# First products of the experts as fp32r products of a rounded half and a remainder, in a deformable convolution with eight experts

## What is computed

```python
# B, C, H, W = 4, 64, 16, 16
def block(x):
    x = x + conv(_ln_c(x))           # deformable 3x3 convolution, 9 taps, bilinear sampling
    t = x.reshape(B, C, H*W).transpose(0, 2, 1)
    t = t + ffn(_ln_t(t))            # per token, over its 64 channels
    return t back in (B, C, H, W)

def ffn(x):                          # 1024 tokens, 8 experts, hidden 256
    top_w, top_i = top_k(x @ Wg + bg, 2)
    w_dense = sum(one_hot(top_i, 8) * softmax(top_w)[..., None], axis=1)
    out = 0
    for e in range(8):
        h = gelu(x @ W1[e] + b1[e])                  # first product: 64 -> 256
        out = out + w_dense[:, e:e+1] * (h @ W2[e] + b2[e])
    return out
```

## Time and profile before

| | us |
|---|---|
| median of 3 runs (108.62 to 109.21) | 108.91 |
| the profiled execution | 108.63 |
| its span | 106.8 |
| TensorE busy in it | 97.6 |
| VectorE busy in it | 69.3 |
| ScalarE busy in it | 50.7 |

### The profile page before, as it was taken

The page is one execution under the profiler, slowest core; times in us unless marked ns, Lnnn a source line. Parts: engine busy times, 40 slices in busy tenths (PEclk is TensorE's granted clock), DMA queues, the critical chain, the costliest instruction groups (busy, mean ns, idle before and its releaser), DMA issues.

```text
span 106.8 us, 1840 instructions
## 1 busy us (share of the span) xinstructions
PE 97.6 (91%) x624; PEld 53.4 (50%) x624; DVE 69.3 (65%) x196; ACT 50.7 (47%) x99; POOL 13.9 (13%) x25
## 2 busy tenths in 40 slices
...
PEclk9999999999999999999999999999999999999999
...
GB/s 73 179 125 367 5 3 0 6 0 0 0 0 6 0 0 0 0 3 6 0 0 0 0 3 0 6 0 0 0 0 0 0 0 6 0 0 0 0 0 98
DMA packets 1976, 2.37 MB, mean 22 GB/s; under 512 B 816, under 2 KB 1456, under 8 KB 1968
## 3 DMA queue, kind: packets, MB, share of 16 engines
...
...
HBM read 2.00 MB, written 0.26 MB: 21 GB/s over the span
## 4 chain that ended last, share of the span: by engine, by line
PE 73%; DVE 13%; issue 6%; ACT 3%; DMA 2%; POOL 1%; DVEq 0%; POOLq 0%
PE taps_ps L674 16%; PE bank_y L746 14%; PE bank_o L688 14%; PE hid_ps L734 9%; PE taps_ps L734 6%; ACT a_sb L350 2%; DMA xt<-in_x_tok 2%; PE hid_ps L661 2%; DVE a_sb L568 2%; PE bank_p L711 2%; DVE xn L529 2%; PE bank_c L724 2%; DVE at L460 2%; PE bank_p L696 1%; PE bank_p L724 1%
## 5 line engine op out<-in xcount | busy, mean ns | idle before, releaser
L674 PE MATMUL taps_ps<-ident,at 128*128 128x128 f32 x144 | 22.5, 283 | 1.6 <-ACT a_sb L350 1.0
L674 PEld LDWEIGHTS taps_ps<-ident,at 128*128 128x128 f32 x144 | 15.5, 142 | 11.0 <-issue 5.0
L460 DVE TENSOR_TENSOR at<-haty,hats 128x768 f32<-128x768 f32 x22 | 20.6, 951 | 0.1
L688 PE MATMUL bank_o<-a_sb,v_sb 128*64 128x256 f32 x144 | 18.1, 386 | 0.6 <-DVE a_sb L568 0.4
L350 ACT ACTIVATE a_sb<-taps_ps 128x512 f32<-128x512 f32 x22 | 12.9, 592 | 7.8 <-PE taps_ps L674 7.8
L382 ACT ACTIVATE hid<-hid_ps,b_col 128x512 f32<-128x512 f32 x20 | 13.1, 682 | 7.3 <-PE hid_ps L734 7.3
L746 PE MATMUL bank_y<-hid,w_sb 128*64 128x512 f32 x64 | 15.4, 604 | 0.0
L594 DVE SCALAR_TENSOR_TENSOR tmp<-bank_y,b_col,spread 128x512 f32<-128x512 f32 x8 | 6.0, 750 | 13.4 <-PE bank_y L746 13.4
L266 POOL TENSOR_TENSOR rs<-ve,power 128x2 f32<-128x2 f32 (+1 forms) x6 | 5.5, 916 | 65.6 <-DVE ve L475 61.4
L688 PEld LDWEIGHTS bank_o<-a_sb,v_sb 128*64 128x64 f32 x144 | 9.8, 136 | 7.1 <-issue 3.2
L568 DVE COPY a_sb<-taps_ps 128x512 f32<-128x512 f32 x14 | 9.5, 686 | 3.0 <-PE taps_ps L674 2.9
...
## 6 DMA issues: line engine op xcount, KB each, us to landing
w_sb<-in_w SPq DMA_DIRECT2D x2, 512.0 KB, 4.1
...
```

The source lines that it names most:

```text
L460: dve.tensor_tensor(at[:, u % AT_RING, j, :, :].rearrange("p k (y x) -> p k y x", x=W), haty[:, b % 2, j, k0:k0 + GROUP, :].unsqueeze(3).b ...
L674: last = pe.transpose(t_bank(step)[:, st * HW + j * P:st * HW + (j + 1) * P], at[:, u % AT_RING, j, k, st * P:(st + 1) * P], ident[:, :])
L688: last = pe.matmul(bank_o[st * O:(st + 1) * O, 0:HW], v_sb[:, img, st, k, :], a_sb[:, slot % A_RING, st, :], start=(k == 0), stop=(k == TA ...
```

## The change

W1 is loaded twice, onto both halves of the partitions, all eight experts side by side. ScalarE rounds it to fp32r (`w1_hi`, four steps whi), and VectorE subtracts to get what is left (`w1_lo`, four steps wlo). Of the tokens, xs now writes x2s as fp32r, rounded, on all partitions, and a new VectorE step xlo overwrites partitions 64 to 127 with the remainder. An H is then, for each of the two experts, two products with all 128 rows accumulated in one bank: `w1_hi` and `w1_lo`, each with the rounded tokens in the upper rows and their remainder in the lower. H waits for wlo and xlo in place of the load and xs. gate reads the same x2s as fp32 over 128 rows, with its weights doubled. xn1 and xn2 become one buffer, ya loses a dimension. The orders of all four engines and the banks are laid anew; which engine makes a copy changes too: osv1 and one more vs are on VectorE, which has 16 of the E copies where it had 14, and xfl1 in place of xfl3. ACT_ORDER has the steps whi2 (behind tanhm1 and ahead of om2), whi1 (behind E2, ahead of abs1), whi0 and whi3 (behind E10 and tanhm2); its beginning is now "xpl0 xfl0 om0 vs0.0 xpl1 vs0.1 abs0 tanhm0 om1 vs1.0 xpl2 vs1.1 xfl2 tanhm1 whi2 om2 E2 whi1 abs1 xpl3". T19 and T20 are both in bank 0 in the new HOMES.

```diff
 PE_ORDER = (
-    "xnT0 conv0 V0.1 omT0 xnT1 V0.0 conv1 V1.1 omT1 T0 xnT2 T1 xnT3 T2 V1.0 M0 T3 T4 conv2 conv3 T5 omT2 T6 T7 V3.0 T8 omT3 T9 M1 "
-    "T10 V2.1 T11 M2 T12 T13 oT0 T14 M3 T15 T16 M4 T17 V2.0 T18 M5 T19 oT1 T20 xT0 T21 M6 T22 xT1 T23 V3.1 T24 gate0 T25 H0.0.0 "
-    "M7 T26 H0.0.1 T27 M8 H0.1.0 T28 wdT0 T29 oT2 T30 sp0.1 T31 M9 H0.1.1 T32 sp0.0 T33 sp0.2 T34 xT2 T35 M10 O0.0 M11 H0.2.0 oT3 "
-    "H0.2.1 O0.1 H0.3.0 xT3 sp0.3 H0.3.1 gate1 O0.2 H1.0.0 H1.0.1 O0.3 H1.1.0 wdT1 H1.1.1 sp1.0 sp1.1 H1.2.0 O1.0 H1.2.1 sp1.2 "
-    "sp1.3 H1.3.0 O1.1 H1.3.1 O1.2 Fa0 O1.3 Fa1 F0 F1 "
+    "xnT0 conv0 V0.0 omT0 xnT1 V0.1 conv1 V1.0 xnT2 omT1 V1.1 T0 conv2 T1 V2.1 T2 omT2 T3 xnT3 T4 M0 T5 T6 M1 T7 T8 conv3 T9 T10 "
+    "V2.0 T11 M2 T12 omT3 T13 V3.1 T14 T15 oT0 T16 M3 T17 M4 T18 M5 T19 V3.0 T20 oT1 T21 M6 T22 xT0 T23 xT1 T24 M7 T25 H0.0.0 T26 "
+    "gate0 T27 M8 T28 H0.0.1 T29 oT2 T30 wdT0 T31 H0.1.0 T32 M9 O0.0 M10 T33 sp0.2 sp0.0 T34 H0.1.1 T35 sp0.1 xT2 M11 H0.2.0 oT3 "
+    "H0.2.1 O0.1 H0.3.0 xT3 H0.3.1 O0.2 H1.0.0 gate1 H1.0.1 sp0.3 H1.1.0 O0.3 H1.1.1 wdT1 H1.2.0 sp1.0 O1.0 sp1.1 H1.2.1 sp1.2 "
+    "O1.1 H1.3.0 sp1.3 H1.3.1 O1.2 Fa0 O1.3 Fa1 F0 F1 "
 ).split()
...
 DVE_ORDER = (
-    "stats0 xn0 stats1 xpu0 sums0 base0 xn1 pos0 dist0 xpu1 xn2 relu0 haty0 first0 xn3 first1 pos1 first2 xpu2 pr1.0 pr1.1 dist1 "
-    "pr2.0 xpu3 xfl3 E4 pr2.1 relu1 haty1 pr3.0 E6 pr3.1 pos2 dist2 E9 pr4.0 pos3 relu2 pr4.1 pr5.0 dist3 E11 pr5.1 E12 st0 haty2 "
-    "vs2.1 pr6.0 E16 E15 pr6.1 pr7.0 E17 pr7.1 lna0 relu3 pr8.0 st1 pr8.1 E21 lna1 haty3 E23 pr9.0 top0 idx0 pr9.1 wd0 pr10.0 "
-    "pr10.1 st2 E31 pr11.0 lna2 E30 pr11.1 E32 E35 tmp0.0 ss0.2 st3 lna3 ss0.3 tmp0.1 top1 tmp0.2 idx1 wd1 tmp0.3 ss1.1 tmp1.0 "
-    "tmp1.1 ss1.2 tmp1.2 tmp1.3 fin0 fin1 "
+    "stats0 xn0 sums0 xpu0 stats1 base0 xn1 xn2 pos0 xpu1 dist0 xfl1 xn3 relu0 haty0 first0 xpu2 pos1 first1 E0 first2 pr1.0 E1 "
+    "pr1.1 dist1 pr2.0 relu1 E3 E4 pr2.1 haty1 vs2.1 pr3.0 pos2 pr3.1 xpu3 pr4.0 E8 dist2 pr4.1 relu2 E9 pr5.0 pr5.1 wlo0 wlo3 "
+    "haty2 pos3 dist3 E13 pr6.0 pr6.1 st0 pr7.0 E16 wlo2 pr7.1 lna0 relu3 haty3 pr8.0 osv1 E19 vs3.0 E18 st1 pr8.1 lna1 pr9.0 "
+    "xlo0 xlo1 pr9.1 pr10.0 E26 pr10.1 top0 idx0 E28 wd0 st2 E31 E30 pr11.0 pr11.1 lna2 E34 E33 ss0.0 wlo1 tmp0.0 xlo2 st3 lna3 "
+    "tmp0.1 xlo3 tmp0.2 top1 idx1 wd1 tmp0.3 ss1.0 tmp1.0 ss1.1 tmp1.1 tmp1.2 ss1.3 tmp1.3 fin0 fin1 "
 ).split()
...
 POOL_ORDER = (
-    "rstd0 rstd1 rstdt0 rstdt1 sel0 rstdt2 rstdt3 ya0.1 ya0.2 ya1.1 ya1.2 "
+    "rstd0 rstd1 sel0 rstdt0 rstdt1 rstdt2 rstdt3 ya0.1 ya1.1 ya0.2 ya1.2 "
 ).split()
...
-        w1_sb = sb("w1_sb", [P, PAIRS, HID])
+        w1_raw = sb("w1_raw", [P, E, HID])
+        w1_hi = sb("w1_hi", [P, E, HID], F32R)
+        w1_lo = sb("w1_lo", [P, E, HID], F32R)
         w2_sb = sb("w2_sb", [P, E, HC, O])
-        wg_sb = sb("wg_sb", [C, E])
+        wg_sb = sb("wg_sb", [P, E])
...
-        x2s = sb("x2s", [P, NB, HW])
+        x2s = sb("x2s", [P, NB, HW], F32R)
...
-            sp.dma_start(wg_sb[:, :], wg).then_inc(ld_wg, 16)
+            for half in range(2):
+                sp.dma_start(wg_sb[half * C:(half + 1) * C, :], wg).then_inc(ld_wg, 16)
             sp.dma_start(bg_bc[:, :], bg.partition_broadcast(P)).then_inc(ld_bias, 16)
             sp.dma_start(b1_col[:, :], b1).then_inc(ld_bias, 16)
             sp.dma_start(b2_col[:, :], b2).then_inc(ld_bias, 16)
-            sp.dma_start(w1_sb[:, :, :], w1).then_inc(ld_w1, 16)
+            for half in range(2):
+                sp.dma_start(w1_raw[half * C:(half + 1) * C, :, :], w1).then_inc(ld_w1, 16)
...
-                    act.activation(x2s[:, b, :], misc(f"xT{b}")[:, 0:HW], ACT.Copy).then_inc(x2s_ready, 1)
+                    act.activation(x2s[:, b, :], misc(f"xT{b}")[:, 0:HW], ACT.Copy).then_inc(x2s_high, 1)
+                elif kind == "whi":
+                    act.wait_ge(ld_w1, 32)
+                    act.activation(w1_hi[:, 2 * b:2 * b + 2, :], w1_raw[:, 2 * b:2 * b + 2, :], ACT.Copy).then_inc(w1_hi_ready, 1)
                 elif kind == "tanhd":
...
+                elif kind == "xlo":
+                    dve.wait_ge(x2s_high, upto(f"xs{b}"))
+                    dve.tensor_tensor(x2s[C:P, b, :], misc(f"xT{b}")[C:P, 0:HW], x2s[C:P, b, :].bitcast(F32),
+                                      ALU.subtract).then_inc(x2s_ready, 1)
+                elif kind == "wlo":
+                    dve.wait_ge(w1_hi_ready, upto(f"whi{b}"))
+                    dve.tensor_tensor(w1_lo[:, 2 * b:2 * b + 2, :], w1_raw[:, 2 * b:2 * b + 2, :],
+                                      w1_hi[:, 2 * b:2 * b + 2, :].bitcast(F32), ALU.subtract).then_inc(w1_lo_ready, 1)
...
-                    take(BANK[step], (x2s_ready, upto(f"xs{b}")))
+                    take(BANK[step], (x2s_ready, upto(f"xlo{b}")))
...
-                            last = pe.matmul(misc(step)[:, t * E:(t + 1) * E], x2s[0:C, i, j * P:(j + 1) * P], wg_sb[:, :], start=True, stop=True)
+                            last = pe.matmul(misc(step)[:, t * E:(t + 1) * E], x2s[:, i, j * P:(j + 1) * P].bitcast(F32), wg_sb[:, :], start=True, stop=True)
...
-                    if h + j + c == 0:
-                        pe.wait_ge(ld_w1, 16)
+                    for half in range(2):
+                        pe.wait_ge(w1_lo_ready, upto(f"wlo{(j + PAIRS * half) // 2}"))
                     for i in (2 * h, 2 * h + 1):
-                        pe.wait_ge(x2s_ready, upto(f"xs{i}"))
+                        pe.wait_ge(x2s_ready, upto(f"xlo{i}"))
                     for half in range(2):
-                        rows = slice(half * C, (half + 1) * C)
-                        last = pe.matmul(two_banks(step)[:, half * 512:(half + 1) * 512], w1_sb[rows, j, c * P:(c + 1) * P],
-                                         x2s[rows, 2 * h:2 * h + 2, :], start=True, stop=True)
+                        dst = two_banks(step)[:, half * 512:(half + 1) * 512]
+                        for part in (w1_hi, w1_lo):
+                            last = pe.matmul(dst, part[:, j + PAIRS * half, c * P:(c + 1) * P], x2s[:, 2 * h:2 * h + 2, :],
+                                             start=(part is w1_hi), stop=(part is w1_lo))
                     last.then_inc(h_done, 1)
...
-        "w1": np.asarray(inputs["L0_ffn_W1"]).reshape(2, PAIRS, C, HID).transpose(0, 2, 1, 3).reshape(P, PAIRS, HID),
+        "w1": np.asarray(inputs["L0_ffn_W1"]).transpose(1, 0, 2),
```

More of the change, by code:

```diff
@@ L64 @@
 HOMES = {
+    'p': (
+        "xnT0 xnT1 xnT2 omT2 conv3 xT0 wdT0 sp0.0 sp0.1 xT3 sp0.3 sp1.1 Fa0 "
+    ),
     'c': (
-        "xnT0 omT0 conv1 xnT2 conv2 omT2 xT0 wdT0 sp0.1 sp0.2 sp0.3 sp1.1 sp1.3 Fa0 "
-    ),
-    'p': (
-        "conv0 xnT1 omT1 xnT3 conv3 omT3 oT0 oT1 xT1 gate0 oT2 sp0.0 xT2 oT3 xT3 gate1 wdT1 sp1.0 sp1.2 Fa1 "
+        "conv0 omT0 conv1 omT1 conv2 xnT3 omT3 oT0 oT1 xT1 gate0 oT2 sp0.2 xT2 oT3 gate1 wdT1 sp1.0 sp1.2 sp1.3 Fa1 "
     ),
     'h': (
-        "V0.1 V0.0 V1.1 V1.0 V3.0 V2.1 V2.0 V3.1 H0.0.0 H0.0.1 H0.1.0 H0.1.1 H0.2.1 H0.3.1 H1.0.0 H1.1.0 H1.2.0 H1.3.0 "
-    ),
-    1: (
-        "T0 T2 T3 T5 T6 T9 T10 T12 T16 T18 T20 T22 T24 T28 T29 T31 T33 T35 "
-    ),
-    0: (
-        "T1 T4 T7 T8 T11 T13 T14 T15 T17 T19 T21 T23 T25 T26 T27 T30 T32 T34 "
+        "V0.0 V0.1 V1.0 V1.1 V2.1 V2.0 V3.1 V3.0 H0.0.0 H0.0.1 H0.1.0 H0.1.1 H0.2.1 H0.3.1 H1.0.1 H1.1.1 H1.2.1 H1.3.1 "
+    ),
+    0: (
+        "T0 T1 T3 T5 T7 T9 T11 T14 T17 T19 T20 T21 T23 T25 T27 T29 T31 T32 T34 T35 "
+    ),
+    1: (
+        "T2 T4 T6 T8 T10 T12 T13 T15 T16 T18 T22 T24 T26 T28 T30 T33 "
     ),
     't': (
-        "H0.2.0 H0.3.0 H1.0.1 H1.1.1 H1.2.1 H1.3.1 "
+        "H0.2.0 H0.3.0 H1.0.0 H1.1.0 H1.2.0 H1.3.0 "
     ),
```

25 lines of the change are left out of this document (13 added, 12 removed), and 10 rows, old and new, of the table ACT_ORDER.

## The result

The changed kernel takes 112.02 us in the median (111.62 to 112.53, four runs) beside 108.95 us for the kernel before (108.62 to 109.21, four runs on the same chip). The ratio is 1.029, with the interval 1.023 to 1.034: 3.07 us more, where +1.4 was forecast and 111.8 was the end of the range. Its profiled execution took 112.23 us, with a span of 110.4.

The account below looks back on a forecast made before the run. VectorE bounds the kernel until about 45 us, then TensorE alone. T20's start 45.5, plus 27.2 to M11, plus 32.85 behind it, gave 105.55 against 104.14: +1.4 us, 110.3 in the median, range 107.5 to 111.8.

Parts of the forecast that it names:

- first0 at 14.35: VectorE's start: first0 begins at 14.35 us instead of 13.49, as xfl1 (0.35) and xn3 (0.52) come ahead.
- ends 20 us before rstdt0: GpSimd: moving sel0 ahead of rstdt0 costs nothing, since sel0 ends 20 us before it.
- The clock drops out of the sum: Whole kernel: the granted TensorE clock stays at the 2.4 GHz level throughout, so it adds nothing.
- T20 at 45.5: T20 starts at 45.5 us instead of 42.87, held by VectorE's queue, where its bank's copy E19 stands behind osv1.
- the floor for TensorE alone, 43.6: T20's start if TensorE were left to itself: 43.6 us, from T0 near 15.2 and 28.54 before, less 0.2 work.
- VectorE in time: Rival: E19 is done by 43.6, TensorE sets the pace to T20; -0.5 us (0.14), -1.8 with fp32 pitch too (0.19).
- T20 to M11, 27.2: TensorE from T20's start to M11's end: 27.2 us instead of 29.0, mainly 1.7 less for shape changes.
- Behind M11, 32.85: TensorE from M11's end to the last product: 32.85 us instead of 32.25, shape changes -0.35, twelve H at +0.08.
- 0.235 a pass: Each H: four one-pass fp32r products at 0.235 us, 0.94 in all, +0.08 each, +1.3 us over sixteen H.
- fp32 pitch: Rival: H's passes follow at 0.215 us as in fp32, 1.3 us less, +0.1 in all; chance 0.18.
- A change of data type costs nothing: TensorE between H and T: data type change alone costs 0; rival, it costs like a shape change, +2.8 us, chance 0.08.
- The remainders, 0.61 each, and the covered edits: VectorE before T20: three wlo at 0.61 us, 1.83 together; whi, xlo, extra loads and other edits hidden, at nothing.

Follow-up runs that it names:

- E1: Not a run: a copy step. With two other early copies moved back from VectorE to ScalarE in the kernel with the old start: 109.37 us, ratio 1.004.
- E3: Not a run: a copy step, moved back from VectorE to ScalarE together with E1 and E8 in the kernel with the old start: 109.37 us.
- E8: Not a run: a copy step, moved back from VectorE to ScalarE together with E1 and E3 in the kernel with the old start: 109.37 us.
- the old start: Changed kernel with sel0 back behind rstdt1 and VectorE's first steps in the order before the change (xfl1, xn3 still ahead of first0): 110.30 us, ratio 1.013.
- E19: Not a run: the copy step, on VectorE behind osv1 in the new order, that frees the bank T20 takes from T19; 0.69 us in the forecast.
- E4: Not a run: a copy step on VectorE ahead of pr4.1, in the kernel before and in the changed one.
- E9: Not a run: the copy step on VectorE that frees the bank of T11.
- the pairs of the kernel with new products: New products in the kernel before's orders, with the two H of an expert pair put together behind M11: 108.45 us, ratio 0.994 to the kernel before.
- those of the old one: Kernel before, no instruction changed, with the two H of an expert pair put together behind M11: 108.22 us, ratio 0.993.

## Why the prediction was wrong

The sign was right, and the sum came near the truth behind the start, in part for a wrong reason; the start was wrong. The experiments form a ladder of medians from the changed kernel down to the one before. It adds up to the 3.07 us because it is made of differences; each step holds the clock as it was in those runs, and is sure to some 0.15 us at best:

| step undone | us | from |
|---|---|---|
| sel0 beside VectorE | 0.67 | 112.02 to 111.35 |
| VectorE's first steps | 1.05 | to 110.30 |
| early copies E1, E3, E8 on VectorE | 0.93 | to 109.37 |
| all that is left | 0.42 | to 108.95 |

The lowest step has the size of the new products in the old orders (109.34), but that is no proof of either: in the new orders the same products win 1.1 us, so what is left of the new orders loses more than that. The forecast's +1.4 is close to the two lower steps, 1.35; the two upper ones weren't in it.

**The start, first0 at 14.35: wrong by 1.05, and this is the step that failed first.** I had written that the new order puts xfl1 and xn3 ahead of first0 "and takes nothing away". Those two cost what I gave them (14.44 with the old start). But I had taken the stretch ahead of them as full and therefore as fixed by its sum, and not looked at the order in it: stats1 filled VectorE's wait for xnT0 and fed a 1.3 us power on GpSimd. Moved behind, it leaves 0.54 us idle and a late xn1. How long that idle time is depends on the warm-up, the 24 products on no data that TensorE makes ahead of xnT0: over all fourteen profiles xnT0 began between 5.67 and 6.80 us, and VectorE is ready for xpu0 at 6.36 in the new order and at 6.86 in the old, so the new one has half a microsecond less to cover such delays.

**sel0 "ends 20 us before rstdt0", at nothing: wrong.** I had looked at the queue it was moved in and at who waits for its result, not at what runs beside it. The Trainium skill, "SBUF — State Buffer", section "SBUF: two separate sides", says that VectorE in certain forms, among them two SBUF inputs against a GpSimd operation that reads SBUF, and GpSimd take one port pair in turn, and that the loser blocks for a whole instruction. The scalar_tensor_tensor of base with 0.63 instead of 0.17 us beside the select, ending with it, agrees. Whether xn, with one tensor read, is slowed by the same thing no row says, but it took 1.57 instead of 1.11 us.

**"The clock drops out of the sum": wrong.** The earlier trace rows show it high in all slices, and I took that for a property of the kernel. It was one of a start in which TensorE stops for 0.92 us at xn1. In the four kernels with a stop of 1.39 us there in their profiles the mean clock was below 0.99 in 13 of 16 runs, with 1.74 in all four; with the 1.39 us filled by small products it did not fall. The kernel before is not free of it: its mean clock was below 0.99 in five of 29 runs on one chip and in six of 29 on another. It isn't the length of one stop alone, since the kernel before stops for 1.38 us at xpu0, at 6 us, and mostly keeps its clock, and since the profile with sel0 back has the 1.39 us and a full clock; there TensorE had worked 2.26 of the 2.5 us up to 7.5, and 1.89 in the changed kernel. What decides is not shown. T0, forecast at 15.2, was at 17.61, and it did not wait for first0, which was done at 16.09, but stood in TensorE's own queue: beside the kernel with the start as before (T0 at 15.42), conv1 began 0.80 us later, behind the late xn1, and from conv1 to T0 it took 4.72 us instead of 3.33, with conv1 and V1.0 at the low clock (0.85 and 0.63 us longer). From T0 on T20 follows in 29.8 to 30.0 us in either.

**T20 at 45.5, because E19 on VectorE stands behind osv1: the number right for the wrong link.** With the start mended it was 45.42, which is luck, and 47.38 is that plus the start. But T20 doesn't wait for VectorE's queue, which was the path that the forecast rested on; without the remainders it moved with T11 alone (0.17 us, for 1.8 us of work taken away). The stops for VectorE's queue are T3, T6 and T11; I had listed the first and the last, and T11 is the last of them. The working went wrong in "Eight copies E stand before T20's release in both": the count is right, and hides that five of them (E0, E1, E3, E4, E8) now stand ahead of pr4.1, where three (E4, E6, E9) did, and E9, which frees the bank of T11, behind all five. Moving three away gave 0.93 us. And the floor for TensorE alone, 43.6, was too low: behind T11 13.92 us pass instead of 13.55, though the stops there, 0.61 in all, are no longer than the 0.73 before; the stretch has 12 changes of shape where it had 10, and one more V. The rival *VectorE in time* fell with it, as VectorE was late, only earlier.

**T20 to M11, 27.2: nearly right.** 27.8, of which 0.54 is the stop for ss0.0 on VectorE, which I had not weighed when I wrote that the new order leaves room. Without it 27.26. The new order has 15 changes of shape there and not the 16 that I counted, which is 0.17 us.

**Behind M11, 32.85: right,** 32.58.

**0.235 a pass: right, and the rival *fp32 pitch* fell.** Records follow each other by 0.23 to 0.24 us and an H takes 0.92 to 0.95; the rule of the Trainium skill ("TensorE: Matmul & The Clock Gate", section "Back-to-back issue gap") that the forecast cites would have given 0.86, and the measurement decides.

**A change of data type costs nothing: right, its rival fell.** A T behind an fp32r H took 0.44 us, as behind another T, and 0.52 once. The shape change at 0.17 held too: 1.12 against 0.92 to 0.95.

**The remainders, 0.61 each, and the covered edits: right but for sel0.** Two wlo in a row took 1.29 us, a whi 0.63, an xlo 0.43. The weights landed 6.3 us after their issue instead of 4.1 and nobody waited; no H waited for wlo or xlo in the changed kernel.

**The range** ended at 111.8 because none of the rivals was a disturbance ahead of T0. All four worked with the products of the experts or with VectorE's queue up to T20.

What stays open: how the 0.83 us that the two moves cost at a full clock divides between them, since both make xn1 late; and how near the 0.9 us is to what the clock costs. And why the pairs of the kernel with new products gain no more than those of the old one isn't separated from the run-to-run spread of some 0.3 us.
